# Seven part-wise transfers in place of eight tile-wise ones for interleaving keys and queries

## The reference

```python
def _attention(q_in, kv_in, Wq, bq, Wk, bk, Wv, bv, mask):
    Q = jnp.einsum('btd,hdk->bhtk', q_in, Wq) + bq[None, :, None, :]
    K = jnp.einsum('bsd,hdk->bhsk', kv_in, Wk) + bk[None, :, None, :]
    V = jnp.einsum('bsd,hdk->bhsk', kv_in, Wv) + bv[None, :, None, :]
    scores = jnp.einsum('bhtk,bhsk->bhts', Q, K) / jnp.sqrt(jnp.asarray(D_K, Q.dtype))
    if mask is not None:
        scores = jnp.where(mask, scores, jnp.finfo(scores.dtype).min)
    attn = jax.nn.softmax(scores, axis=-1)
    out = jnp.einsum('bhts,bhsk->bhtk', attn, V)
    return out.transpose(0, 2, 1, 3).reshape(q_in.shape[0], q_in.shape[1], -1)
```

## Time and profile before

| what | value |
|---|---|
| median of 3 runs | 2833.17 us (2823.28 to 2837.1) |
| profiled execution, its own time | 2817.95 us |
| its span, first to last instruction | 2815.7 us |
| mean granted clock of TensorE | 0.923 |
| PE, PEld busy | 84%, 59% of the span |
| DVE, ACT busy | 54%, 54% |
| POOL busy | 19% |
| transfers q_int<-q_nat | 256, 128 KB each, 2.7 us to landing |
| transfers k_int<-k_nat | 256 (128 KB or 77 KB), 2.7 and 2.3 us |
| transfers q_int<-m_sb | 256, 4 KB each |

### The profile page before, as it was taken

One profiled execution on the slowest core, in us unless ns is written; L12 is line 12 of the kernel. 1 busy time (PEld: TensorE's weight loads), 2 busy tenths in 40 slices (PEclk: granted clock), 3 DMA queues, 4 the chain that ended last, 5 costly groups with the idle time before them and its releaser, 6 DMA issues. The chain is left out here.

```text
span 2815.7 us, 69952 instructions
## 1 busy us (share of the span) xinstructions
PE 2378.0 (84%) x27712; PEld 1661.4 (59%) x27712; DVE 1529.4 (54%) x4449; ACT 1521.5 (54%) x2379; POOL 545.7 (19%) x730
## 2 busy tenths in 40 slices
PE   3656989898989989898989989898989989897975
PEld 2434647575666657575666657575666657564743
DVE  3343555657465565657465565657465565635232
ACT  1324545665665565665656555665656565644442
POOL 2111112121212122121212222121212122121111
PEclk9655979999999999999999999999999999998986
DMA  2100010101010110101010110101010110110000
GB/s 113 34 16 13 22 29 19 33 24 43 23 44 24 29 33 19 33 23 44 23 44 24 29 33 19 33 23 45 23 44 24 28 32 21 33 29 17 17 20 17
DMA packets 103753, 84.22 MB, mean 30 GB/s; under 512 B 15001, under 2 KB 102682, under 8 KB 102938
## 3 DMA queue, kind: packets, MB, share of 16 engines
q1 hardware_dynamic: 103449, 79.91, 11.6%
HBM read 14.21 MB, written 4.19 MB: 7 GB/s over the span
## 5 line engine op out<-in xcount | busy, mean ns | idle before, releaser
L990 DVE TENSOR_REDUCE smax<-by_query_banks 128x8 f32<-128x616 f32 (+1 forms) x512 | 516.0, 1008 | 345.9 <-PE by_query_banks L1309 345.2
L776 ACT ACTIVATE probs<-by_key_banks 77x1024 f32<-77x1024 f32 (+1 forms) x480 | 485.4, 1011 | 160.2 <-PE by_key_banks L1332 156.6
L1246 PEld LDWEIGHTS by_key_banks<-moe_w,hid 128*128 128x128 f32 x4096 | 476.0, 192 | 14.1
L1246 PE MATMUL by_key_banks<-moe_w,hid 128*128 128x128 f32 x4096 | 483.7, 275 | 0.0
L757 ACT ACTIVATE hid<-by_query_banks,cols 128x512 f32<-128x512 f32 x512 | 335.0, 687 | 274.8 <-PE by_query_banks L1237 273.0
L1380 PE MATMUL weighed_bank<-probs,values 128*32 128x128 f32 x8192 | 356.5, 296 | 5.9 <-ACT probs L776 2.7
L1309 PE MATMUL by_query_banks<-k_int,q_int 32*128 32x128 f16 (+1 forms) x4096 | 198.2, 218 | 170.1 <-DVE smax L990 87.9
L1309 PEld LDWEIGHTS by_query_banks<-k_int,q_int 32*128 32x128 f16 x4096 | 120.6, 98 | 334.7 <-issue 215.4
L1380 PEld LDWEIGHTS weighed_bank<-probs,values 128*32 128x32 f32 x8192 | 206.7, 115 | 96.8 <-issue 44.5
L770 ACT ACTIVATE m_sb<-turned_bank 16x128 f16<-16x128 f32 x256 | 67.9, 265 | 293.9 <-PE turned_bank L1362 293.9
L1332 PE MATMUL by_key_banks<-q_int,k_int 32*128 32x128 f16 x3840 | 206.0, 230 | 9.2 <-ACT probs L776 7.0
(11 more groups left out here) (237 smaller groups left out, 3905.0 us busy)
## 6 DMA issues: line engine op xcount, KB each, us to landing
q_int<-q_nat SPq DMA_DIRECT2D x256, 128.0 KB, 2.7
k_int<-k_nat SPq DMA_DIRECT2D x128, 128.0 KB, 2.7
k_int<-k_nat SPq DMA_DIRECT2D x128, 77.0 KB, 2.3
x_tok<-in_x SPq DMA_DIRECT2D x17, 256.0 KB, 3.0
q_int<-m_sb SPq DMA_DIRECT2D x256, 4.0 KB
out<-res SPq DMA_DIRECT2D x16, 256.0 KB, 2.3
ctx_tok<-in_ctx SPq DMA_DIRECT2D x17, 154.0 KB
hid<-in_moe_w SPq DMA_DIRECT2D x1, 2048.0 KB
```

The costliest lines, as they stand in the source:

```text
L776: act.activation(probs[h % 2][0:nk], pair[0:nk], ACT.Exp, scale=DH ** -0.5)\
L990: dve.tensor_reduce(smax[h // 2 % 2][:, pair, :], scores, AX.X, ALU.max, negate=True)\
L1246: last = pe.matmul(B[e % 2][:, seq_tok(b)], hidden[e % 2][:, c, seq_tok(b)], moe_w2[:, e, c, :], start=(c == 0), stop=(c == CHUNKS - 1))
```

## The change

The columns of the weights (and biases) of keys and queries are reordered on the host (`spread`), so that partition 4r + j of `k_nat` holds feature 32j + r. One part (128 partitions) can then be written by a single transfer into every fourth row of `k_int`, for all four tiles. The parts: k high to rows 0 and 2, k low to row 1; q high to rows 0 and 1, q low to row 2. The constant rows are written once at the start from a new tile `lines`, eight transfers ahead of the experts' weights; the zero in row 3 of each head, which the maxima overwrite, is renewed by a seventh, small transfer (4 partitions of 4 rows). `k_nat` and `q_nat` shrink from four parts to two. The copies on POOL are gone. One semaphore `shift` counts all seven transfers; PE waits for it once, before unit 0.

```diff
-PER |= {f"shift_{j}": 2 * 16 for j in range(TILES)} | {f"m_shift_{j}": 16 for j in range(TILES)}
+PER |= dict(shift=7 * 16) | {f"m_shift_{j}": 16 for j in range(TILES)}
...
-        k_nat = sb("k_nat", [P, PARTS, N], F16)
-        q_nat = sb("q_nat", [P, PARTS, N], F16)
+        k_nat = sb("k_nat", [P, 2, N], F16)
+        q_nat = sb("q_nat", [P, 2, N], F16)
+        lines = sb("lines", [P, 2, N], F16)
...
-                 (ln_eps[:], LN_EPS), (minus_half[:], -0.5), (k_nat[:, 3, :], MAX_SCALE), (q_nat[:, 3, :], 0.0)]
+                 (ln_eps[:], LN_EPS), (minus_half[:], -0.5)]
+        fills = [(lines[:, 0, :], MAX_SCALE), (lines[:, 1, :], 0.0)] + fills
...
+            sp.wait_ge(s_fill, 2)
+            for m, x in enumerate(att):
+                sp.dma_start(x.k_int[3::PARTS, :, :], lines[:, 0, 0:GROUP * KEYS[m]]).then_inc(s_lines, 16)
+                sp.dma_start(x.q_int[3::PARTS, :, :], lines[:, 1, :]).then_inc(s_lines, 16)
             for dst, src in expert_loads:
...
                 yield f"proj{m}"
+                sp.wait_ge(S["proj_sb"], at(g, "proj_sb", 1))
+                sp.dma_start(x.k_int[0::PARTS, :, :], k_nat[:, 0, 0:keys]).then_inc(S["shift"], 16)
+                sp.dma_start(x.k_int[2::PARTS, :, :], k_nat[:, 0, 0:keys]).then_inc(S["shift"], 16)
+                sp.dma_start(x.q_int[3::32, :, :], lines[0:16, 1, :]).then_inc(S["shift"], 16)
                 sp.wait_ge(S["low"], at(g, "low", 1))
-                sp.wait_ge(S["dup"], at(g, "dup", 1))
-                sp.dma_start(x.k_int[:, 0, :], k_nat[0:32, :, 0:keys]).then_inc(S["shift_0"], 16)
+                sp.dma_start(x.k_int[1::PARTS, :, :], k_nat[:, 1, 0:keys]).then_inc(S["shift"], 16)
                 yield f"query{m}"
+                sp.wait_ge(S["proj_sb"], at(g, "proj_sb", 2))
+                sp.dma_start(x.q_int[0::PARTS, :, :], q_nat[:, 0, :]).then_inc(S["shift"], 16)
+                sp.dma_start(x.q_int[1::PARTS, :, :], q_nat[:, 0, :]).then_inc(S["shift"], 16)
                 sp.wait_ge(S["low"], at(g, "low", 2))
-                sp.wait_ge(S["dup"], at(g, "dup", 2))
-                sp.dma_start(x.q_int[:, 0, :], q_nat[0:32, :, :]).then_inc(S["shift_0"], 16)
-                for j in range(1, TILES):
-                    sp.dma_start(x.k_int[:, j, :], k_nat[rows_of(j), :, 0:keys]).then_inc(S[f"shift_{j}"], 16)
-                    sp.dma_start(x.q_int[:, j, :], q_nat[rows_of(j), :, :]).then_inc(S[f"shift_{j}"], 16)
+                sp.dma_start(x.q_int[2::PARTS, :, :], q_nat[:, 1, :]).then_inc(S["shift"], 16)
...
-            def twice(r, m):
-
-                keys = GROUP * KEYS[m]
-                g = r.projections[m]
-                yield f"proj{m}"
-                pool.wait_ge(S["proj_sb"], at(g, "proj_sb", 1))
-                pool.sem_inc(s_waited, 1)
-                pool.tensor_copy(k_nat[:, 2, 0:keys], k_nat[:, 0, 0:keys]).then_inc(S["dup"], 1)
-                yield f"query{m}"
-                pool.wait_ge(S["proj_sb"], at(g, "proj_sb", 2))
-                pool.sem_inc(s_waited, 1)
-                pool.tensor_copy(q_nat[:, 1, :], q_nat[:, 0, :]).then_inc(S["dup"], 1)
...
                 if not g.first:
-                    for j in range(TILES):
-                        act.wait_ge(S[f"shift_{j}"], at(g.before(), f"shift_{j}"))
+                    act.wait_ge(S["shift"], at(g.before(), "shift"))
...
-                dve.scalar_tensor_tensor(q_nat[:, 2, :], X[0][:], col(f"bq{m}"), q_nat[:, 0, :],
+                dve.scalar_tensor_tensor(q_nat[:, 1, :], X[0][:], col(f"bq{m}"), q_nat[:, 0, :],
...
-                    if c % 2 == 0:
-                        pe.wait_ge(S[f"shift_{j}"], at(source, f"shift_{j}"))
+                    if c == 0:
+                        pe.wait_ge(S["shift"], at(source, "shift"))
...
             pe.wait_ge(s_fill, filled)
+            pe.wait_ge(s_lines, 16 * 2 * len(att))
...
+    spread = np.arange(D).reshape(TILES, D // TILES).T.reshape(-1)
+    for m in range(4):
+        for w in "qk":
+            mat[f"w{w}{m}"] = mat[f"w{w}{m}"][:, spread]
+            col[f"b{w}{m}"] = col[f"b{w}{m}"][spread]
```

More of the change, by code:

```diff
@@ L182 @@
 PER = dict(scores=COUPLES, smax=COUPLES, m_t=TILES, m_sb=TILES, scores_t=COUPLES, probs=COUPLES, pv=COUPLES,
-           o_sb=BLOCKS, o_t=BLOCKS, o_rden=BLOCKS, o_norm=BLOCKS, proj=3, proj_sb=3, low=2, dup=2,
+           o_sb=BLOCKS, o_t=BLOCKS, o_rden=BLOCKS, o_norm=BLOCKS, proj=3, proj_sb=3, low=2,
            on_t=1, on_sb=1, attn=1, attn_sum=1, ln=9, rs=2, turn=1, feat=1)
-PER |= {f"shift_{j}": 2 * 16 for j in range(TILES)} | {f"m_shift_{j}": 16 for j in range(TILES)}
+PER |= dict(shift=7 * 16) | {f"m_shift_{j}": 16 for j in range(TILES)}
 PER |= {f"ln_{n}": 9 for n in ("ctx", "x", "cross", "l1")} | {f"rs_{n}": 2 for n in ("ctx", "x", "cross", "l1")}
@@ L211, in build @@
         s_fill = ctx.enter_context(nc.semaphore("filled"))
+        s_lines = ctx.enter_context(nc.semaphore("constant_lines_in"))
         s_held = ctx.enter_context(nc.semaphore("held"))
@@ L592, in light @@
                     pool.tensor_tensor(res3[:], res3[:], shifted(shift31), ALU.add).then_inc(S["res31"], 1)
-                    yield from twice(r, CROSS3)
                 yield "value3"
@@ L616, in light @@
                     pool.tensor_tensor(x_sa[:], x_sa[:], row("sa_out_b"), ALU.add).then_inc(S["sa_res"], 1)
-                    yield from twice(r, SELF2)
                 if r.b:
@@ L621, in light @@
                     pool.tensor_tensor(x_s3[:], x_s3[:], row("bo_s"), ALU.add).then_inc(S["s3_res"], 1)
-                    yield from twice(r, SELF3)
                 if r.f:
@@ L646, in light @@
                     pool.tensor_tensor(x_ca[:], x_ca[:], row("ca_out_b"), ALU.add).then_inc(S["ca_res"], 1)
-                    yield from twice(r, CROSS2)
             def go(r):
```

## The result

The changed kernel takes 2814.03 us in the median of 20 runs (2808.75 to 2823.49), the kernel before 2829.14 us (2816.87 to 2837.1, 20 runs). The ratio is 0.995 with a 95% interval of 0.9938 to 0.9963: 14 to 15 us faster. It stands on the edge of the 0.5% that "same" was to mean, towards the side that was given 0.20. The gain is about four times the forecast 3.8 us, so the middle of the forecast was missed although the range holds.

What follows compares the result with a forecast made beforehand. Transfers were taken as hidden except in the first and last attention, PE otherwise trading turns with DVE and ACT. +2.7 - 0.5 - 5 - 1 = -3.8 us from a median of 2833.17 gave 2829, full range 2806 to 2850.

Steps and rivals of the forecast that it cites:

- same: Whole kernel: a time within 0.5% (14 us) of 2833, given 0.66; faster had 0.20, slower 0.14.
- What bounds the kernel: Whole kernel: transfers hidden in all but two of 64 attentions; in between PE trades turns with DVE and ACT.
- The two exposed places: First and last attention, where PE sits idle until the seventh transfer lands: +1.4 and +1.3 us, sum +2.7.
- the fill: Start of the kernel: eight constant-line transfers ahead of the expert weights, hidden by 3 us; +3 if that cover went.
- Row of maxima: Steady loop: the m_sb transfer goes out up to 2.6 us earlier on SP's queue; -0.5 us, between -1 and 0.
- GpSimd's copies: Experts, once a turn: without the 128 copies DVE's l_hat no longer collides; -1 us, between -3.8 and 0.
- Waits that PE no longer executes: Score units 2, 4 and 6: 192 satisfied waits go, 0.09 us each in 70 units; taken as -5 us.
- The clock: Steady loop: 1.09 us per hundredth of granted clock and turn; no term in the sum, only in rival 1 and Rival 2.
- rival 1: Steady loop: less PE idling between score units keeps the clock up; 2792, or 2812 for half the turns; chance 0.20.
- Rival 3: New-form transfers: pieces spread over 4 engines, not 16, delay the exposed places and m_sb; about 2863; chance 0.04.
- Rival 2: First score units after experts and the pass boundary: lower clock makes it slower, 2857 or 2853; chance 0.10.
- Rival 4: PE's score units: the priced waits hide in the ping-pong with ACT; about 2835; chance 0.66 together with the forecast.

Runs made afterwards that it cites:

- e3: The changed kernel with GpSimd's 128 copies put back, writing a spare tile that nothing reads: 2810.6 us.
- e9: The changed kernel with PE's 192 satisfied waits for shift put back before units 2, 4 and 6, called after the wait for smax: 2809.6 us.
- e12: The kernel before, with only PE's wait for smax called ahead of its wait for shift_j before units 0, 2, 4 and 6: 2808.7 us.
- e5: The changed kernel with PE's wait for shift executed before every one of an attention's eight units, called ahead of smax: 2829.3 us.
- e1: The changed kernel with PE's 192 satisfied waits for shift put back before units 2, 4 and 6, called ahead of smax: 2825.9 us.
- e11: e4 with calls turned round where PE waits for two semaphores, so that the late one stands on the matmul: 2792.5 us.
- e4: The changed kernel with the turned unit's waits moved behind the first two score matmuls, causal attention excepted: 2803.3 us.

## Why the prediction was right and wrong

**What bounds the kernel** was right: the transfers are hidden in all but two attentions, and PE's turns with DVE are where a change shows.

**The two exposed places**: forecast +1.4 and +1.3, measured +0.8 and +0.6. The count of steps was right; the seventh transfer takes 2.15 us to PE, not 2.63, so PE's two waits are 3.1 and 3.3 us and not the 4.2 that I had named. Together with the fill it is 2.4 us against 2.7, by luck, for **the fill** was wrong: "hidden by 3 us" was +1.0. I gave the lines' pieces a place after the weights; but 234 of their 1024-byte pieces move between 11 and 12 us, beside the last weights, and `fc_aug` landed 1.0 us later, at 12.35.

**Row of maxima**: -0.5, too small to be told by any run here.

**GpSimd's copies**: -1 was 0. The collision is real and comes back in e3, and DVE's busy time fell by 11 us where I had counted 3.8, but DVE is not waited for there. (`l_hat` still reached 0.466 us twice where I had said 0.34 throughout.) Rows that show a longer instruction show no cost until someone waits for it.

**Waits that PE no longer executes**: -5. At equal clock the kernels are some 5 us apart, and with 2.4 us lost at the ends and in the fill the waits gave some 7.6; counted in the trace, 76 late starts at 0.09 us are 6.8. The 0.09 us per unit was read rightly, 0.14 and 0.05 stand in the rows of before and after; 70 units at 0.09 (6.3) was nearer than the 5 that I took. But the reason was wrong. I wrote that a satisfied wait "is always satisfied, but not free"; e9 and e12 show no cost of it there, and they show that the 0.09 us are paid where the late semaphore sits on the instruction ahead and not on the matmul.

**The clock** is the step that failed: it stands in the sum with nothing, and it is the larger part of the gain. I named its mechanism as rival 1 (faster, 2812) and argued against it with "0.3 us a turn is little". The mean granted clock rose from 0.915 to 0.9206, worth 8 of the 13 to 15 us. The prediction also took the profiled execution's offset from the median (15.2 us, of three runs) over to the changed kernel unaltered; that offset is mostly the clock of that one execution (0.923 against 0.915 on average), and the changed kernel's own profile lies only 3.5 us below its median. What stays open is why the clock rises. With more delay e5 has no lower clock than e1, and I have one profile of each kernel, so I can show for e11 that the low stretches are shorter, not what makes them so.

**Rivals.** Rival 3 (four engines): refuted, seven issues stand 0.635 us apart and the last lands sooner. Rival 2 (slower by the clock) did not occur; the clock went the other way. Its threshold had a slip: 14 / 12 / 1.09 is 1.1 hundredths of clock, not 1.2. Rival 4 (the waits hide) is excluded by e1.

What would have found the cause: asking which of the two semaphores PE's matmul itself waits for. That stands in PE's order ahead of the prediction, as `[waits smax,shift_1]`, `smax` first.

## What to carry to other kernels

Where an instruction waits for two semaphores, look in the built order which of them it holds itself. The one that comes last should be that one, and the one that has long been met should stand ahead of it; turning two calls round gave some 20 us here, more than a rewrite of the transfers. A wait belongs in front of the first instruction that needs it, not at the start of a group (e4, 11 us, with 119 waiting instructions fewer). And a profile's time compares with another's only together with its clock: take the mean clock over all runs before you put a difference down to instructions.

## What the runs showed of the hardware that was not expected

- Where the late wait is on an instruction of its own ahead of the matmul, PE starts 0.14 us after `smax` ends; where the matmul holds it itself, 0.05 to 0.06 us (e1, e9, e12). The waiting instruction takes 0.05 us.
- Pieces of 1024 bytes, which only keys and queries (and the constant lines) have, took 0.072 us of an engine in the mean in the tile-wise form (32 partitions of four rows into 128) and 0.047 in the part-wise one (128 into every fourth), with a median of 0.046 in both: some pieces of the tile-wise form take far longer than most. Issue to PE's start fell from 2.63 to 2.15 us. Why was not tried.
- TensorE's half-clock stretches stand at the same two places of nearly every turn. In the changed kernel turns with 6.8 us each and turns with 3.4 us each mostly alternate; in e11, with the same matmuls, eleven of twelve turns have 3.4 us each. The mean granted clock of the kernels here ranged from 0.9114 (before, on one chip) to 0.9285 (e11).
